# Householder tridiagonalisation on one core: a new order of each step's short instructions, and dummy matmuls placed and counted differently

## What is computed

```python
def _L0_gnn_ref(features, A, W1, b1, W2, b2):
    deg = jnp.sum(A, axis=0) + jnp.sum(A, axis=1) - jnp.diagonal(A)
    d_inv_sqrt = jnp.where(deg > 0, jax.lax.rsqrt(deg), 0.0)
    L = jnp.diag(deg) - A
    L_norm = d_inv_sqrt[:, None] * L * d_inv_sqrt[None, :]
    _, U = jnp.linalg.eigh(L_norm)
    ...
```

## Time and profile before

| | |
|---|---|
| median of 3 runs | 4024.7 us (4023.17 to 4032.79) |
| the profiled execution's own time | 4029.76 us |
| its span | 4027.7 us |
| TensorE matmul busy | 3257.0 us (81%) |
| VectorE busy | 3095.7 us (77%) |
| ScalarE busy | 1644.8 us (41%) |
| GpSimd busy | 55.7 us (1%) |
| granted TensorE clock, mean | 0.899 of full speed |

### The profile page before, as it was taken

One profiled execution on the slowest core, in us unless ns is written; L12 is line 12 of the kernel. 1 busy time (PEld: TensorE's weight loads), 2 busy tenths in 40 slices (PEclk: granted clock), 3 DMA queues, 4 the chain that ended last, 5 costly groups with the idle time before them and its releaser, 6 DMA issues. The chain is left out here.

```text
span 4027.7 us, 66622 instructions
## 1 busy us (share of the span) xinstructions
PE 3257.0 (81%) x16975; PEld 2163.7 (54%) x17214; DVE 3095.7 (77%) x19300; ACT 1644.8 (41%) x6492; POOL 55.7 (1%) x71
## 2 busy tenths in 40 slices
PE   5999999999999999888967666455048899998859
PEld 4777777776777777556634222343024443554347
DVE  7999998888887777998889899999964314455467
ACT  3555554444444444444423322112113315554545
POOL 0000000000000000000000000000000000120000
PEclk8999999999999999998788888555569999999969
DMA  0000000000000000000000000000020000000001
GB/s 11 2 2 2 2 2 2 2 1 2 1 2 2 1 2 2 2 1 1 1 1 1 0 1 1 1 1 1 0 72 1 0 0 0 0 0 0 0 6 38
DMA packets 14176, 16.74 MB, mean 4 GB/s; under 512 B 571, under 2 KB 10214, under 8 KB 13798
## 3 DMA queue, kind: packets, MB, share of 16 engines
q1 hardware_dynamic: 13798, 12.48, 1.2%
HBM read 8.28 MB, written 4.19 MB: 3 GB/s over the span
## 5 line engine op out<-in xcount | busy, mean ns | idle before, releaser
L207 PE MATMUL ps<-zero_stream 128*128 128x512 bf16 x1745 | 541.9, 388 | 6.2 <-issue 0.2
L229 PE MATMUL ps<-vectors,UT 128*128 128x128 f32 x2482 | 388.9, 290 | 0.0
L229 PE MATMUL ps<-vectors,U 128*128 128x128 f32 x2366 | 375.4, 292 | 1.0 <-DVE vectors L505 0.3
L229 PEld LDWEIGHTS ps<-vectors,UT 128*128 128x128 f32 x2482 | 313.7, 192 | 23.5 <-DVE vectors L505 23.5
L229 PEld LDWEIGHTS ps<-vectors,U 128*128 128x128 f32 x2366 | 301.8, 193 | 24.0 <-DVE vectors L505 24.0
L343 ACT ACTIVATE vectors<-WihT,refl 128x4 f32<-128x4 f32 (+2 forms) x383 | 115.5, 302 | 393.8 <-DVE refl L467 393.8
L325 ACT ACTIVATE refl<-ps,tiny 128x1 f32<-128x1 f32 x511 | 133.8, 262 | 284.9 <-PE ps L234 180.9
L207 PEld LDWEIGHTS ps<-zero_stream 128*128 128x128 bf16 x1966 | 212.5, 122 | 54.9 <-issue 19.8
L705 ACT ACTIVATE sturm_signs<-sturm_products,sign_bias 128x576 bf16<-128x576 f32 x96 | 74.6, 777 | 352.7 <-DVE products_mark L732 352.7
L223 PE MATMUL ps<-vectors,ident 128*128 128x22 f32 (+4 forms) x1022 | 190.7, 267 | 22.2 <-DVE vectors L501 22.0
L1750 ACT ACTIVATE gates<-ps,gate_bias 128x512 f32<-128x512 f32 (+1 forms) x252 | 152.8, 637 | 130.8 <-PE ps L1737 95.8
(11 more groups left out here) (616 smaller groups left out, 8356.3 us busy)
## 6 DMA issues: line engine op xcount, KB each, us to landing
out_dram<-x SPq DMA_DIRECT2D x16, 256.0 KB, 2.3
adj<-in_adj_dram SPq DMA_DIRECT2D x1, 1024.0 KB, 5.1
l2w_in<-in_L_gnn_W_dram SPq DMA_DIRECT2D x2, 128.0 KB
Wqkv<-in_L_gnn_Wqkv_dram SPq DMA_DIRECT2D x1, 192.0 KB
L_gnn_W<-in_L_gnn_W_dram SPq DMA_DIRECT2D x2, 64.0 KB
L_gnn_Wg<-in_L_gnn_Wg_dram SPq DMA_DIRECT2D x2, 64.0 KB
x<-in_x_dram SPq DMA_DIRECT2D x4, 0.5 KB
L_gnn_Wo<-in_L_gnn_Wo_dram SPq DMA_DIRECT2D x1, 64.0 KB
```

The lines of the kernel that those rows point to most:

```text
L207: nc.tensor.matmul(psum[t][:],still[:,0:P],still[:],start=False,stop=True,skip_group_check=True)
L229: ins=nc.tensor.matmul(ax(m)[:,o:o+WIDE],A[version(m)%2][:,t,j*P:(j+1)*P],XG[:,t,X_:X_+1].broadcast_to([P,WIDE]),start=t==NT-1,stop=t==b)
```

## The change

In the first block (r==0) the denominator goes ahead of the reflector and waits for ScalarE's shift itself; the inverses and x_by_shift go ahead of the last rows of y. In the second (r==1) twice_norm goes ahead of the sign, corrections ahead of the reflector, x_by_shift ahead of the last rows of y, and on TensorE the pair sums stand behind the first tile of the product instead of behind all but the last. In the last (else) twice_norm, signed_unit, by_dots, shift, reflector, corrections, denominator follow one another, ahead of the column and y. The dummy matmuls of the last block become 2 and 1 (1 and 1 in steps with an update), and one more stands right behind the norm's matmul. The third block stays as it is. No instruction is added or removed but the dummy matmuls.

```diff
--- before.py
+++ after.py
@@ -157,7 +157,7 @@
     return range(NT-1 if regime(m)==3 else NT-2,NT)
 def streams(m):
 
-    if regime(m)==3: return (3 if update_tile(m) else 4,1)
+    if regime(m)==3: return (1 if update_tile(m) else 2,1)
     return (1 if update_tile(m) or ends_panel(m) else 2,2)
 def still_tile(m):
 
@@ -258,7 +258,7 @@
                         if r==2: pair_products(m)
                         if r==0: pair_sums(m)
                         if r==1:
-                            product(m,NT-1,range(NT-1,b,-1)); pair_sums(m); product(m,NT-1,range(b,b+1))
+                            product(m,NT-1,range(NT-1,NT-2,-1)); pair_sums(m); product(m,NT-1,range(NT-2,b-1,-1))
                         product(m,NT-2)
                         if ends_panel(m): transposed(m//PANEL-1)
                         if update_tile(m): updated(*update_tile(m))
@@ -275,6 +275,7 @@
                         pe.wait_ge(e_ready,m-TAIL+1)
                         if m==TAIL: pe.wait_ge(kap_ready,m-1)
                         nc.tensor.matmul(NORM[:,0:2],XG[:,NT-1,X_:X_+1].broadcast_to([P,P]),XG[:,NT-1,E_:X_+1],start=True,stop=True).then_inc(s2_ps,1)
+                        streamed(m,1)
                         pe.wait_ge(ub_ready,m-1); pe.wait_ge(w_ready,m-1)
                         pair_products(m)
                         product(m,NT-1)
@@ -460,7 +461,8 @@
                         k.inc(nc.vector.tensor_tensor_reduce(out=sq[:,0,sl],in0=V[:,sl,i],in1=y,scale=1.0,scalar=0.0,op0=ALU.mult,op1=ALU.add,accum_out=dp[:,0:1]))
                         nc.vector.tensor_tensor_reduce(out=sq[:,1,sl],in0=V[:,sl,i],in1=cc,scale=1.0,scalar=0.0,op0=ALU.mult,op1=ALU.add,accum_out=dp[:,1:2]).then_inc(dp_ready,1)
                     def denominator():
-                        if r>0: after("S")
+                        if r==0: v.wait_ge(s_ready,m)
+                        else: after("S")
                         mark("N2",nc.vector.scalar_tensor_tensor(out=col(N2_),in0=col(S_),scalar=ALPHA,in1=col(S_),op0=ALU.add,op1=ALU.mult))
                     def inverses():
                         after("N2")
@@ -485,18 +487,18 @@
                         pair_parts()
                         v.wait_ge(A_copied,copies_of(version(m))); v.wait_ge(xrow_ps,m)
                     if r==0:
-                        multiply(1); inverse(); multiply(1); sign(); by_both(); corrections(); reflector(); column_of_A()
-                        first_rows_of_y(); denominator(); last_rows_of_y(); inverses(); dot_parts(); x_by_shift(); y_below(); x_scaled(); y_scaled(); p_column()
+                        multiply(1); inverse(); multiply(1); sign(); by_both(); corrections(); denominator(); reflector(); column_of_A()
+                        inverses(); first_rows_of_y(); x_by_shift(); last_rows_of_y(); dot_parts(); y_below(); x_scaled(); y_scaled(); p_column()
                     elif r==1:
-                        multiply(1); inverse(); sign(); twice_norm(); by_both(); shift(); reflector(); corrections(); denominator(); column_of_A()
-                        first_rows_of_y(); inverses(); last_rows_of_y(); x_by_shift(); dot_parts(); y_below(); x_scaled(); y_scaled(); p_column()
+                        multiply(1); inverse(); twice_norm(); sign(); by_both(); shift(); corrections(); reflector(); denominator(); column_of_A()
+                        first_rows_of_y(); inverses(); x_by_shift(); last_rows_of_y(); dot_parts(); y_below(); x_scaled(); y_scaled(); p_column()
                     elif r==2:
                         by_rows(); inverse(); sign(); twice_norm(); by_dots(); shift(); corrections(); reflector(); denominator()
                         v.wait_ge(A_copied,copies_of(version(m))); column_of_A(); last_rows_of_y(); inverses(); y_below(); x_by_shift(); y_scaled(); x_scaled(); p_column()
                     else:
                         v.wait_ge(ds,row_at[0])
-                        by_rows(); inverse(); sign(); by_dots(); twice_norm(); signed_unit(); corrections(); reflector(); shift()
-                        column_of_A(); last_rows_of_y(); denominator(); inverses(); y_below()
+                        by_rows(); inverse(); sign(); twice_norm(); signed_unit(); by_dots(); shift(); reflector(); corrections(); denominator()
+                        column_of_A(); last_rows_of_y(); inverses(); y_below()
                         v.wait_ge(u_ready,m)
                         nc.vector.tensor_scalar(XG[:,sl,G_+2*slot(m)],V[:,sl,i],col(T0),None,ALU.mult).then_inc(ub_ready,1)
                         x_by_shift(); y_scaled(); x_scaled()
```

## The result

The changed kernel takes 4064.27 us (median of 4 runs, 4063.39 to 4064.97) against 4026.39 us (4023.17 to 4032.79) for the kernel before, a ratio of 1.0086 with an interval of 1.0059 to 1.0112: slower by 0.9%, 38 us. The forecast was 4052 us, with a range of 4012 to 4086. The profiled execution has 4063.39 us, a span of 4061.4 us and a mean granted clock of 0.859 instead of 0.899.

What follows compares the result with a forecast made beforehand. VectorE's short instructions and L268 bound the first two blocks; VectorE at 2.4 GHz, TensorE with dummies at 1.2 GHz, the last. 4029.8 us + 22 (first) - 18 (second) + 18 (last) gave 4052 us, range 4012 to 4086.

Steps and rivals of the forecast that it cites:

- +22, -18 and +18: Forecast changes in us: first block slower by 22, second faster by 18, last slower by 18.
- L268 as releaser in most steps: First block: expected sign that L505 comes about 0.2 us further behind the sign, released by the dot parts' matmul.
- The discount of 18 steps: First block: 18 steps where L505 already waits long for L268 hide the delay, leaving 109 steps x 0.2 us.
- rival three: First block costs nothing because A x is late there; whole 4030 us, chance 0.13.
- The bound of -28: Second block: largest gain, 128 x 0.22 us, what the sums' matmul gains.
- 70 steps of 3.67 us and 57 of 3.04: Last block: 70 of 127 steps at 1.2 GHz, the others at 2.4 GHz, 430 us together, 18 more than 412.
- each stretch at 1.2 GHz lasts 17 to 24 us as in the earlier trace: Last block: slow stretches last 5 to 6.5 steps of 3.67 us, putting some 6 steps in 11 at 1.2 GHz.
- the forecast's own range: Last block: 50 to 100 slow steps, whole kernel 4035 to 4075 us; the forecast's chance 0.57.
- rival two: Last block stays at 1.2 GHz throughout: +54 us instead of +18, whole 4088 us, chance 0.12.
- 4.10 - 0.43: Last block at 1.2 GHz: TensorE bounds the step, which falls by one dummy matmul to 3.67 us.
- I take 0.08: Last block at 2.4 GHz: us saved per step by the new VectorE order, from an estimated 0.06 up to 0.11.
- Rival one: Last block: the clock holds with four dummies, gaining 16 to 26 us; whole 4018 down to 4008 us, chance 0.18.

Runs made afterwards that it cites:

- the order alone: The kernel before with only the last block's new VectorE order, its dummy matmuls as before: 3997.98 us, ratio 0.9931.
- the dummies alone in the old order: The kernel before with only the changed number and place of the last block's dummy matmuls: 4064.45 us, ratio 1.0088.
- the best version: The kernel before plus last block's new order with old dummies, second block's early sums and new order, x_by_shift behind dot parts there: 3959.76 us, ratio 0.9807.

## Why the prediction was right, and where its terms were off

The sign and the range held, and the forecast's terms were +22, -18 and +18 where +23.9, -20.6 and +30.6 were measured. 12 us of the 38 were missed, nearly all in the last block.

**First block: right, by its mechanism.** (The 121 instructions of the window in the earlier trace rows bound 120 steps, so a step took 4.60 us before, not 4.57; it takes 4.80 now.) x_by_shift starts 0.26 us behind the inverses (0.27 forecast) and the last rows of y come 0.27 later (0.28). L507 comes 0.20 us later in an ordinary step, as forecast. L268 releases it: it ends at 305.96 + 0.38 = 306.34, and L507 starts at 306.38. The mark that I had named, L268 as releaser in most steps, isn't in the view of L507's idle time, because an instruction of VectorE still runs there (L472, from 306.16 to 306.38) and that time doesn't count as idle; the row has the same 18 steps as the earlier trace rows:

```profile
  PE ps L268: 6.1, 18
```

The discount of 18 steps was wrong. 15 of them are the steps that end a panel, and by the starts of L505 and L507 these lose 0.27 us in the mean, more than the others with 0.19; one of the 18 lies in the second block. All 120 steps of the window lose 0.20 in the mean, which makes the 24. Moving x_by_shift back brings the block to 555.6 us; rival three, that the first block costs nothing, has fallen.

**Second block: right, its size within 3 us.** The inverses come 0.32 us earlier (medians; 0.33 forecast), the dot parts 0.14 (0.14), and L507 0.16 instead of 0.14. The bound of -28 that I named, what the sums' matmul gains, is what the early sums give in the old order.

**Last block: that the clock falls was right, that it comes back was wrong, and two errors cancel in part.** I forecast 70 steps of 3.67 us and 57 of 3.04, together 430.

- The share of steps at 1.2 GHz. The step that failed is "each stretch at 1.2 GHz lasts 17 to 24 us as in the earlier trace rows". The fall came after six steps, where about five had been reckoned, but those lengths had been measured with five dummies. With four the clock didn't come back in 425 us, so 122 steps were slow, more than the 50 to 100 of the forecast's own range, and the block's clock is 0.52, not "near 0.7". That is the course of rival two, to which I had given 0.12. (The kernel before had 17 steps with three dummies ahead of L285, not 16: its trace has 34 instructions of L218 in the block, two for each. That changes nothing in the sum.) 52 more steps at a difference of about 0.45 us make +23.
- The step at 1.2 GHz: 425.30 / 122 = 3.49 us, not 3.67; 70 x 0.18 makes -13. The changed kernel's TensorE timeline in that stretch shows why.

```profile
1804.63 0.43 PE L277 MATMUL ps<-vectors 128*128 128x2 f32 x2
1804.91 0.59 PE L207 MATMUL ps<-zero_stream 128*128 128x512 bf16 x1
1805.29 0.44 PE L243 MATMUL ps<-vectors 128*128 128x12 f32 x2
1805.58 0.77 PE L229 MATMUL ps<-vectors,UT 128*128 128x128 f32 x2
1806.15 1.06 PE L207 MATMUL ps<-zero_stream 128*128 128x512 bf16 x2
1807.00 0.42 PE L286 MATMUL ps<-vectors,WihT 128*128 128x2 f32 x2
...
1808.10 0.43 PE L277 MATMUL ps<-vectors 128*128 128x2 f32 x2
```

I had counted 4.10 - 0.43, two dummies less ahead of the dot product and one more behind the norm, each at 0.43. The two removed are worth 0.86. But L243 starts only 0.38 us behind the early one, which has L243's old place behind L277, and from L243 to L229 it is now 0.29 us where the kernel before had 0.43 at this clock, in the two rows between those of the earlier trace rows:

```profile
1851.12 0.57 PE L243 MATMUL ps<-vectors 128*128 128x8 f32 x2
1851.55 0.77 PE L229 MATMUL ps<-vectors,U 128*128 128x128 f32 x2
```

So it costs 0.38 - 0.14 = 0.24, and 4.10 - 0.86 + 0.24 = 3.48. The weight loads (PEld) of L243, before and after, fit this:

```profile
1851.05 0.55 PEld L243 LDWEIGHTS ps<-vectors 128*128 128x128 f32 x2
...
1804.92 0.72 PEld L243 LDWEIGHTS ps<-vectors 128*128 128x128 f32 x2
```

Before, they start 0.07 us ahead of the matmul; now 0.37 ahead, beside the dummy. That this is where the 0.14 comes from is my reading; no run took it apart.

- The step at full clock: 2.99 us, not 3.04. "I take 0.08" for the new order was low; by the starts of L505 it is 0.13, in the mean of the steps at full clock (3.12 before, 2.99 with the order alone) as in their median (3.06 and 2.93). Here almost no step was left to have it: the 17.5 us ahead of the fall stand where 5 steps of 3.04 stood in the sum, +2. With the order alone it makes some 17 of the 29 us that the block gains (127 x 0.13); the rest goes with fewer falls.

430 + 23 - 13 + 2 = 442 us, where 442.8 were measured. That the time lies in the range is in part luck: rival two, whose course came, stood at 4088 us, above the range's end of 4086, and its price of +54 was too high by the same 0.18 us a step. Two errors of opposite sign, too few slow steps and too dear ones, left the sum 12 us from the forecast. Rival one, that the clock holds, decided the other way; its ground, that one dummy in an early pause would do for two at the end, is refuted by the dummies alone in the old order. The clock fell at 1634.70, behind steps whose longest pause of TensorE was 0.37 us (one stands below, in brackets), and stayed down with the matmuls busy for 417.47 of 425.30 us (the row stands in the last section). The Trainium skill, TensorE: Matmul & The Clock Gate, section on HAM oscillation, puts falls of the clock down to long idle gaps between bursts of matmuls. This case's trace doesn't agree, since no such gap stands ahead of the fall.

```profile
1628.66 0.39 PE L286 MATMUL ps<-vectors,WihT 128*128 128x2 f32 x2 [0.37 <-DVE vectors L447]
```

## What to carry to other kernels

When dummy work holds a clock, price its removal with the clock gone for good as well as by past falls, and change their number alone before bundling it with an order that helps. On an engine that works through its list in order, an instruction that waits for a result just started holds up all behind it: x_by_shift ahead of the last rows of y cost 20.8 us in the first block and 16 in the second, and behind the dot parts these were gone. Take such a change apart by stretch before it is kept or dropped whole: this one held +24 us in the first block, -21 in the second, -29 by the last block's order (382.9 - 412.2) and +60 by its dummies (442.8 - 382.9). The last two hang on each other: in the old order the same dummies cost 450.9 - 412.2 = 39, and the new order then gives only 450.9 - 442.8 = 8.

## What the runs showed of the hardware that was not expected

- The busy share of TensorE's matmuls over a stretch doesn't tell the clock that they got. From its fall on, the changed kernel's last block has 417.47 of 425.30 us busy at 0.50 (second row below); the best version has 337.09 of 378.90, at 1.00. Matmuls at half the clock take longer and so look busier. Only stretches at the same clock compare: ahead of its fall the changed kernel has 14.65 of 17.50 us, 84% (first row), and the best version 89%. The columns are those of the best version's last row.

```profile
1617.20:1634.70 17.50, 14.65 (x88) 9.90 (x89) 16.09 (x136) 8.58 (x47) 0.00 (x0) 1.00 0.00 1
1634.70:2060.00 425.30, 417.47 (x1693) 349.59 (x1727) 331.54 (x2788) 169.32 (x924) 0.00 (x0) 0.50 0.00 1
```

- The lower clock costs less than dummies that fail to hold it: in the new order, a step without dummies takes 3.17 us at 1.2 GHz, a step with five 2.98 at 2.4 GHz (378.9 / 127 in the best version), and a step with four 3.49 at 1.2 GHz.
- With the same dummies the falls differ from one execution to the next. The last block is the same code in the order alone and in the best version, and their profiled executions have 13.7 us at 0.50 and none. In the kernel before, with steps of 3.07 us, it was 64.9; that a shorter step has fewer falls would fit, but one profiled execution each doesn't show it. Why the clock doesn't come back with four stays open.
